# First tile of a two-layer graph kernel: which queue issues which load, and in what order

## The reference, cut to what matters

```python
def _cxin_conv(x, a, eps, W, b):
    ax = a @ x
    h = ax + (1.0 + eps[0]) * ax
    for i in range(3):
        h = relu(h @ W[i].T + b[i])
    return h
x1 = layernorm(x + concat(_cxin_conv(x, adj, ...), _cxin_conv(x2, adj, ...)) @ Wm.T + bm)
out = layernorm(x1 + mamba(layernorm(relu(adj @ x1 @ gcn_w + gcn_b))))
```

## Time and profile before

| | |
|---|---|
| Median of three runs | 1144.08 us |
| Profiled execution | 1143.51 us, span 1141.6 us |
| VectorE busy | 1036.0 us, 91% of the span |
| TensorE busy | 984.3 us, 86% |
| ScalarE busy | 527.2 us, 46% |
| GpSimd busy | 295.3 us, 26% |
| Moved by DMA | 226.37 MB, mean 198 GB/s |

### The profile page before, as it was taken

How to read it: one execution, slowest core, us unless ns; L and a number is a source line. 1 busy time by engine, 2 the same in 40 slices (tenths; PEclk the granted TensorE clock), 3 DMA queues, 4 the chain that set the end, 5 groups by cost and what they waited for, 6 DMA issues and landing times. The chain is left out here.

```text
span 1141.6 us, 13185 instructions
## 1 busy us (share of the span) xinstructions
PE 984.3 (86%) x4162; PEld 677.3 (59%) x4162; DVE 1036.0 (91%) x858; ACT 527.2 (46%) x946; POOL 295.3 (26%) x197
## 2 busy tenths in 40 slices
PE   0689999999999999999988979979889799685555
PEld 0567777777777877444555646646556465463444
DVE  1999999999999999724999999999999999999994
ACT  1343343434444342324555555736456556564431
POOL 5321112020202110102323224332333243322340
PEclk9999999999999999999999999999999999896776
DMA  9999999999999999847444253254441542101100
GB/s 263 225 178 304 332 330 347 322 349 326 326 355 321 352 329 310 189 180 257 159 158 166 94 203 133 72 207 146 164 182 61 202 147 75 38 20 55 38 9 10
DMA packets 190908, 226.37 MB, mean 198 GB/s; under 512 B 8624, under 2 KB 164336, under 8 KB 176528
## 3 DMA queue, kind: packets, MB, share of 16 engines
q1 hardware_dynamic: 105920, 163.60, 43.9%
q10 hardware_dynamic: 81856, 54.80, 18.8%
q0 software_dynamic: 3088, 7.47, 2.1%
HBM read 162.66 MB, written 63.18 MB: 198 GB/s over the span
## 5 line engine op out<-in xcount | busy, mean ns | idle before, releaser
L807 DVE STREAM_TRANSPOSE at<-rows 128x1024 f32<-128x1024 f32 x136 | 267.7, 2009 | 21.6 <-DMA rows<-in_adj 8.4
L507 POOL TENSOR_TENSOR dBuP<-dtu,b_sb 128x1024 f32<-128x1024 f32 x64 | 153.5, 2398 | 397.5 <-DVE hs L960 227.5
L1025 PE MATMUL yT<-ah,xh 128*128 128x512 f32 x512 | 211.1, 412 | 47.8 <-DVE al L815 42.7
L547 ACT ACTIVATE ah<-at 128x2048 fp32r<-128x2048 f32 x64 | 122.5, 1915 | 210.2 <-PE yT L1025 208.6
L1112 PE MATMUL bank<-adjc,xm 128*128 128x512 f32 x448 | 210.7, 599 | 1.6 <-ACT axT L625 1.6
L1025 PE MATMUL yT<-ah,xl 128*128 128x512 f32 x512 | 200.5, 392 | 0.0
L1025 PE MATMUL yT<-al,xh 128*128 128x512 f32 x512 | 200.5, 392 | 0.0
L1196 PE MATMUL yT<-ident,pr 128*128 128x128 f32 x1024 | 152.5, 299 | 38.0 <-DVE pr L967 38.0
L714 ACT ACTIVATE dA<-dt,A_sb 128x512 f32<-128x512 f32 x256 | 169.7, 713 | 26.2 <-DVE dt L914 26.0
L1196 PEld LDWEIGHTS yT<-ident,pr 128*128 128x128 f32 x1024 | 132.2, 154 | 65.0 <-DVE pr L967 51.4
L967 DVE TENSOR_TENSOR pr<-hs,bank 128x1024 f32<-128x1024 f32 x128 | 153.0, 1196 | 3.9 <-PE bank L1192 3.8
(11 more groups left out here) (150 smaller groups left out, 994.2 us busy)
## 6 DMA issues: line engine op xcount, KB each, us to landing
adjT<-at SPq DMA_DIRECT2D x56, 1024.0 KB, 7.8
adjc<-adjT SPq DMA_DIRECT2D x56, 1024.0 KB, 5.0
rows<-in_adj SPq DMA_DIRECT2D x152, 256.0 KB, 8.3
rows<-in_adj ACTq DMA_DIRECT2D x136, 256.0 KB, 8.8
b_sb<-b_dram ACTq DMA_DIRECT2D x32, 512.0 KB, 3.7
xm<-in_x SPq DMA_DIRECT2D x4, 512.0 KB, 16.2
xs<-in_L_gnn_x ACTq DMA_DIRECT2D x4, 512.0 KB, 17.1
res<-in_x POOLq DMA_DIRECT2D x8, 256.0 KB, 7.2
```

What stands on the lines that cost most here:

```text
L507: nc.gpsimd.tensor_tensor(dBu(n, par)[:, :, 1:], dtu[par][:, :, :], b_sb[pair % 2][:, nB(n) % 2:nB(n) % 2 + 1, :].to_broadcast([P, H, TILE ...
L547: nc.scalar.activation(ah[c % 2][:, :], at[c % 2][:, :, :].rearrange("p m t -> p (m t)"), ACT.Copy)\
L807: last = nc.vector.transpose(dst.rearrange("p m (g i) -> p g m i", i=32), src.rearrange("p g (i m) -> p g m i", i=32))
L1025: last = mm(acc[k][:, :], w[:, b, :], v[c % 2][:, cols], start=(b == 0 and j == 0), stop=(b == KB - 1 and j == 2))
```

## The change

ScalarE issues five loads only: quarters 2 and 3 of piece 0, part 0 of x2, quarters 2 and 3 of piece 1. SyncE issues all four quarters of pieces 2 and 3. Parts 1 to 3 of x2 go to GpSimd's queue, between the loads of small weights, with no wait for x ahead of them; the large weights come behind part 3. VectorE takes the low part of piece 0 behind `x_lo(0)`, ahead of the transpose of piece 1.

```diff
@@ SyncE
             for c in range(NROWS):
-                load_rows(sp, (0, 1), 0, c)
+                load_rows(sp, (0, 1) if c < 2 else range(Q), 0, c)
                 load_x(sp, x, 0, c)
@@ GpSimd
-            for k in range(2):
-                pool.wait_ge(x_in[k], 16)
-            load(w_nat[:, 0:LAYERS, :], W1.rearrange("l o d -> o l d"))
-            load(w_nat[:, LAYERS:2 * LAYERS, :], W2.rearrange("l o d -> o l d"))
-            load(w_nat[:, 2 * LAYERS:, :].rearrange("p k d -> p (k d)"), Wm)
             for k, b in enumerate((b1, b2)):
                 for l in range(LAYERS):
                     load(bias_sb[:, k, l:l + 1], b[l].rearrange("(p o) -> p o", o=1))
+            load_x(pool, x2, 1, 1)
             load(eps_sb[:, 0:1], eps1.partition_broadcast(P))
...
-            load(bm_sb[:, :], bm.partition_broadcast(P))
             load(gcn_b_sb[:, :], gcn_b.rearrange("(p o) -> p o", o=1))
-            load(gcn_w_sb[:, :], gcn_w)
...
-            load(w_in_sb[:, :], w_in)
+            for h in range(H):
+                for dst, src in ((conv_b_sb, conv_b), (b_dt_sb, b_dt), (D_sb, D_skip)):
+                    load(dst[:, h:h + 1], src.rearrange("(h p o) -> h p o", h=H, o=1)[h])
+            load_x(pool, x2, 1, 2)
             load(conv_w_sb[:, :, :], conv_w.rearrange("(h p) k -> p h k", h=H))
...
             load(A_sb[:, :, :], A_log.rearrange("(h p) s -> p h s", h=H))
+            load_x(pool, x2, 1, 3)
+            load(w_nat[:, 0:LAYERS, :], W1.rearrange("l o d -> o l d"))
+            load(w_nat[:, LAYERS:2 * LAYERS, :], W2.rearrange("l o d -> o l d"))
+            load(w_nat[:, 2 * LAYERS:, :].rearrange("p k d -> p (k d)"), Wm)
+            load(bm_sb[:, :], bm.partition_broadcast(P))
+            load(gcn_w_sb[:, :], gcn_w)
+            load(w_in_sb[:, :], w_in)
             load(w_out_sb[:, :, :], w_out.rearrange("(h p) d -> p h d", h=H))
...
@@ ScalarE
-            for c in range(NROWS):
-                load_rows(act, (2, 3), 0, c)
-                load_x(act, x2, 1, c)
+            load_rows(act, (2, 3), 0, 0)
+            load_x(act, x2, 1, 0)
+            load_rows(act, (2, 3), 0, 1)
             act.preload_act_table_set("natural_log_exp_and_others")
@@ VectorE
                     if not mlp and c == 0:
                         x_lo(0)
-                    if c > 1 or c > 0 and not mlp:
+                        lo(it, 0)
+                    if c > 1:
                         lo(it, c - 1)
```

More of the change, by code:

```diff
@@ L416, in _ @@
             load(A_sb[:, :, :], A_log.rearrange("(h p) s -> p h s", h=H))
+            load_x(pool, x2, 1, 3)
[5 more added lines that the diff above has]
+            load(w_in_sb[:, :], w_in)
             load(w_out_sb[:, :, :], w_out.rearrange("(h p) d -> p h d", h=H))
-            for h in range(H):
-                for dst, src in ((conv_b_sb, conv_b), (b_dt_sb, b_dt), (D_sb, D_skip)):
-                    load(dst[:, h:h + 1], src.rearrange("(h p o) -> h p o", h=H, o=1)[h])
             v = w_xp.rearrange("(h p) j -> p h j", h=H)
```

## The result

The changed kernel takes 1148.38 us in the median of 14 runs (1142.81 to 1150.79), the kernel before, run beside it, 1142.91 in 14 (1141.43 to 1146.64). The ratio is 1.0039, with a 95% interval from 1.0028 to 1.0050: 4.5 us slower. I had forecast 1139.3, 4.8 us faster, with 1134.0 to 1144.3 as the range and 0.08 for slower.

A forecast was written before the change was run, and what follows sets the result against it. VectorE was taken as the chain after a late start; with rows of pieces 2 and 3 in at 34.0 and 40.4 us, piece 4 moves from 51.36 to 46.6, a gain of 4.8 us from 1144.08 to 1139.3, range 1134.0 to 1144.3.

The forecast's parts named there:

- What bounds the kernel: VectorE is the chain from 27.17 us on; the shift of piece 4's transpose, at 51.36, carries to the end.
- ScalarE's queue: At the start, with five loads kept, ScalarE is free at 5.1 us instead of 26.1 and rounds x at 12.2.
- VectorE's order: Low part of piece 0 ahead of piece 1's transpose costs nothing; al ready by 18.4 us, TensorE starts 17 us earlier.
- The bytes ahead: 8.52 MB must be through before piece 2's rows are in, 1.04 less than the 9.56 before.
- The rate: Loads in the first 38 us keep the mean 264 GB/s; piece 2's rows in at 34.0 us, piece 3's at 40.4.
- rival C: SyncE's queue alone at 179 GB/s for stretches takes nearly all back; gain 0.6 us, 1143.5; chance 0.29.
- Rival D: SyncE's queue at its lone pace throughout, piece 4's rows land at 53 to 55, 1145.5 to 1148 us; chance 0.08.
- GpSimd's queue ahead of the rest: GpSimd's x2 parts and all weights, 1.57 + 1.18 MB, come ahead of the rows of piece 2.
- x2 on GpSimd isn't late: No delay taken for x2 from GpSimd's issuing beside VectorE; its parts go out at about 4.7, 11.4 and 14.5 us.
- a sign of being wrong: The forecast is wrong if idle time sits elsewhere, above all if ScalarE waits for x part 1 beyond 22 us.
- The low part ahead of piece 4 at 2.3: VectorE's low part, 3.46 us before, takes 2.3 since GpSimd's subtraction falls beside the transpose; otherwise 1.2 us are gone.

The follow-up runs named there:

- e4: Changed kernel, with ScalarE issuing its rows of piece 4 (and so of 5) only when the rows of piece 2 are in; 1143.12 us, one run.
- e1: Changed kernel, with GpSimd's large weights held until the rows of piece 3 are in; 1146.93 us, one run.
- e5: Changed kernel, with rows of pieces 2 and 3 split again, quarters 0 and 1 on SyncE, 2 and 3 on ScalarE; 0.9966 of the kernel before.
- e2: Changed kernel, with ScalarE loading quarters 0 and 1 and SyncE 2 and 3 for pieces 4 and 5 of the first tile; 1150.34 us, one run.
- e3: Changed kernel, with only the columns of adj read exchanged for pieces 4 and 5 of the first tile, partitions written kept; 1148.67 us, one run.
- e7: Kernel before, with SyncE loading quarters 0 and 2 and ScalarE 1 and 3 in the first tile; 1149.59 us, one run.
- e10: Changed kernel, pieces 2 and 3 split over SyncE and ScalarE, ScalarE's piece 3 after piece 0's rounding, large weights held for piece 2's rows; 0.9950 of the kernel before.
- e8: Changed kernel, with TensorE's first matmul held until piece 2 is turned; 1148.18 us, one run.

## Why the prediction was wrong, point by point

- **What bounds the kernel: right.** The shift at piece 4 (+4.5) is the shift of the next tile (+4.7) and of the last scan (+4.3).
- **ScalarE's queue: right.** 5.0 against 5.1 us for the end of its issues and table; rounding at 11.0, where I had 12.2.
- **VectorE's order: right, the time of piece 1 in part by luck.** al of piece 0 was done at 17.1, 1.3 us before the forecast, but piece 1 was turned at 18.8 (18.4 forecast), since it waited 1.7 us for its rows, which I had in at 17.
- **The bytes ahead: right.** 8.52 MB forecast, 8.9 moved in 38.5 us, with about the same 0.4 too little as in the kernel before, and piece 2 turned at 38.9.
- **The rate: wrong, and this is the step that failed.** "The mean rate over the first 38 us is 264 GB/s, over the first 32 us 263, so that a MB more or less moves a landing by 3.8 us." That mean belongs to a kernel in which the two queues' rows always go to opposite halves of the partitions; it is a property of the order that the change takes away. In its place stand some 180 GB/s where SyncE's rows are alone (187 in e4) or both queues are at the same half (180 in the changed kernel). The term was mis-sized by 4.9 us at piece 2 (34.0 forecast, 38.9), by 7.9 at piece 3 (40.4, 48.3) and by 9.3 at piece 4 (46.6, 55.9), where I had even the rows of piece 4 in by 44.4.
- **The row was there.** The earlier trace rows shows 179 GB/s for one queue, and I read it as what a queue can do alone, good for ten us in rival C and for all in rival D. e4 shows that a second queue beside it changes nothing as long as it is at the same half. Rival D had the sign, and nearly the place (53 to 55 for the rows of piece 4, turned at 55.9), with 0.08. Its mechanism, three queues served one after the other, is not what happened: from 22 to 27 us GpSimd's and SyncE's queues ran side by side at 302 GB/s, and from 28 to 34 us SyncE's and ScalarE's did. But two queues that share the rate of one cost as much as two in turn, and that is why its sum came near.
- **GpSimd's queue ahead of the rest: right in kind, too small in size.** From 22 to 27 us it moved 1.27 MB and SyncE's 0.23. e1 puts the whole cost of the weights at 7.8 us at piece 2, where their bytes at 264 GB/s are 4.5, and at 5.6 us at piece 4.
- **x2 on GpSimd isn't late**: its second part goes out at 5.2 and what ScalarE waits for is SyncE's x part 1, until 22.65. That is 0.65 us beyond the 22 that I had named as a sign of being wrong; it costs VectorE 1.0 us, and it is not what the loss comes from.
- **The low part ahead of piece 4 at 2.3: right** (2.25), and for the reason given: GpSimd's subtractions (45.8 to 50.5 us) were over before it began at 52.2.

Of the two ways in which the change touches the loads, the whole pieces on SyncE cost 11.1 us at piece 4 (55.87 - 44.81, e5), net of what ScalarE's longer issuing in e5 takes, and everything else in it together is worth 6.6 us there (51.36 - 44.81). The difference is the loss of 4.5.

The Trainium skill, page "SBUF — State Buffer", section "Door 1: The DMA port swizzle (why `[64,N]` ≈ `[32,N]`)", says that partitions 0 to 63 are reached over one half of the ports of the DMA and 64 to 127 over the other, so that 64 partitions get no more than 32. The rows here agree: 180 to 200 GB/s for one half, by one queue or by two, and in places less (150 in e2). The same page of the Trainium skill, section "Can I just issue two DMAs to hit both halves?", has a load at each half at only 6% over a single one; here the pair gets 285 to 290 GB/s where one queue alone gets 183, 56 to 58% more, and the measurement decides. I had looked at this page of the Trainium skill for the port of GpSimd and VectorE and passed over the rule that spoke against the change.

## What to carry to other kernels

A mean DMA rate read from a profile holds for the mix of transfers that made it. Before moving a load to another queue, look which partitions the transfers write that will run side by side: two queues of 32-partition loads were worth 290 GB/s here at opposite halves (below and above partition 64) and 180 to 200 at the same one. And when a change makes an engine ready earlier for data, ask first when the data will be there: here 10.6 us won at piece 1 were worth nothing, because the rows of pieces 2 to 4 set the time.

## What the runs showed of the hardware

- The rate of these loads of rows depends on the partitions written, not on the columns read (e3: 186 GB/s with the columns exchanged), and at one half not on the number of queues (e4: 183 GB/s for one queue, 180 for two in the changed kernel). Two full queues at opposite halves: 289 (before), 290 (e5), 285 (e4), 276 (e1, 35 to 37 us). Same half: 180 (changed), 200 (e7), 150 (e2, 37 to 42 us, the lowest; why it is below 180 is open).
- Opposite halves helped only while both queues ran side by side. From 46.5 to 48.5 us of the kernel before 739 of 769 packets are ScalarE's, and the rate is 191 GB/s; from 45 to 75 us, where the queues often take turns like this, the mean is 174.
- A queue with large packets takes the larger part: from 22 to 27 us of the changed kernel 469 packets of GpSimd's queue and 471 of SyncE's went through, one for one, but 1.27 MB against 0.23, since its packets hold 2.7 KB in the mean and those of the rows 0.5 KB.
- Slower queues hold the engine that issues: in e7 the same twelve loads kept ScalarE 4.1 us longer.
- A subtraction on GpSimd with both inputs in SBUF stretches VectorE's from 2.25 to as much as 4.4 us (e10). VectorE's then ends 2.15 us behind GpSimd's (44.97 after 42.82, 60.71 after 58.56 in e10), about its own length, as if it had run only once the other was over.
- TensorE's granted clock stood at 1.2 GHz (0.50 of full speed) from 34 to 38 us of the changed kernel, where it had multiplied piece 0 from 17.2 to 24.9 us and then done nothing. In e8, where it had done nothing at all since the start, its first matmuls from 44.1 us on came 0.43 us apart too, as under 1.2 GHz, though the window shows 1.00; from 47.2 us on they came 0.23 us apart, as under 2.4 GHz. Neither moved the tile.
